# First attention on one core: the attends moved behind the second maximum, the token turn and the first projection

## The chip, the cores and the metric

The kernel runs on one core of a Trainium2 chip. The metric is the device time of one execution in microseconds, the median of the runs shown. The engines are TensorE (PE, with its weight loads as PEld), VectorE (DVE), ScalarE (ACT), GpSimd (POOL) and SyncE (SP). Each works through its own instructions in the order in which they are written, and semaphores join them.

## The reference

Two layers of attention and mixture-of-experts feed-forward on 16 sequences of 256 tokens and 128 features, each part wrapped in layer norms. Only the first attention matters here; it has 16 heads of 8 features and runs two passes, in which the first pass's result is the second pass's query:

```python
        x = (hidden_states - mu) * jax.lax.rsqrt(var + EPS_LN) * ln_w + ln_b
        q = (x @ Wq + bq).reshape(B, S, NH, HD)
        k = (x @ Wk + bk).reshape(B, S, NH, HD)
        v = (x @ Wv + bv).reshape(B, S, NH, HD)
        q = _l2norm(q)
        k = _l2norm(k)
        state = q
        for _ in range(STEPS):
            sim = jnp.einsum('bqhd,bkhd->bqhk', state, k)
            att = jax.nn.softmax(BETA * sim, axis=-1)
            state = jnp.einsum('bqhk,bkhd->bqhd', att, v)
        o = state.reshape(B, S, H) @ Wo + bo
        return residual + o
...
    x = x + _layernorm(_L0_attn_ref(_layernorm(x, axis=-1), ...), axis=-1)
    x = x + _layernorm(_L0_ffn_ref(_layernorm(x, axis=-1), ...), axis=-1)
    x = x + _layernorm(_L1_attn_ref(_layernorm(x, axis=-1), ...), axis=-1)
    x = x + _layernorm(_L1_ffn_ref(_layernorm(x, axis=-1), ...), axis=-1)
    return x
```

## The kernel before

The first attention (`first_attention`) works in units of one sequence (batch b) and four heads: 64 units, one unit started in each step k. In step k, with b = k // 4 and r = k % 4, the engines work on several units at different depths. The order on each engine is written out by hand; a step on TensorE holds:

- op (L449), the output projection of batch b-2, in steps r=3
- S1 (L400): the first pass's scores of unit k into `ps_s`, four banks; ScalarE's exponentials 0 and 1 (L541, `exps`) read it into `p1`
- m0 (L411, `maxima`): the first of four matmuls that score the second pass's queries of unit k-3, for whose maxima VectorE waits (L651). m0, m1, m2 and m3 write the two banks `ps_d` in turn with qp, kp, vp, op, lg, place and O
- yT (L431, r=2): out2 of batch b-2 turned into `ps_a`, copied by ScalarE (L547) between exponentials 0 and 1
- A (L418, `attend`): the attends of units k-6 (second pass, `p2`) and k-1 (first pass, `p1`) into `ps_o`, 16 matmuls written as 32 in the trace. They need last step's exponentials (`exp_done`) and a copied `ps_o` (`o_copied`), and announce `o_full`, on which ScalarE's copy to `ot` (L577) waits
- xT (L431, r=2): the normalised tokens `z1` of batch b+3, turned into `ps_a`. It waits for `z1_ready` (VectorE, L610, shown as a_z) and for ScalarE's copy of yT out of `ps_a`
- qp (L437, r=3): the query projection of batch b+3, read by VectorE at L635
- m1, then S2 (L400): the second pass's scores of unit k-5 into the same `ps_s`, once exponentials 0 and 1 have read it; ScalarE's exponentials 2 and 3 read them
- m2, T (the turned queries, copied by ScalarE between exponentials 2 and 3), lg or place, m3, kp, zT, vp, O (L524, `ot` turned, read by VectorE at L765 to L779), KQ (L425), and S1 of the next step, which waits for exponential 3.

A writer of a `ps_d` bank waits (`wait_d`) until VectorE has read the tile before last: m1 waits for O of the step before in r=0 and r=1, for the reader of m0 where qp stands between them (r=3), for op's reader where it doesn't (r=3 of batches 13 to 15). On VectorE m0's maximum in r=3 stands behind y (L669, reads op) and the scaling of the last projected batch (L686), which needs POOL's powers (L822). A writer of `ps_a` waits (`wait_a`) until ScalarE has copied the tile before. On ScalarE the copy of `ot` (L577) stands ahead of the xT activation (L580) and of exponential 2. Routing work on VectorE (`choose`, `place`) comes at the end of some steps.

Of the kernel before, what the change touches and what calls it, by code (L numbers as in the profile page):

```python
# [20 lines left out]
ACT = mybir.ActivationFunctionType  # L21
# [4 lines left out]
B, S = 16, 256  # L26
# [167 lines left out]
def first_attention(nc, X, Z, ident, a):  # L194
# [22 lines left out]
    def unit(n):  # L217
        return 0 <= n < UNITS
# [4 lines left out]
    with ExitStack() as ctx:  # L223
# [10 lines left out]
        z1 = sb("z1", [P, TPB, D])  # L234
# [23 lines left out]
        xT = sb("xT", [P, S])  # L258
# [10 lines left out]
        ps_o, ps_a = pb("ps_o", [P, 512]), pb("ps_a", [P, 512])  # L269
# [5 lines left out]
        a_full, a_done = sem("a_full"), sem("a_done")  # L275
# [19 lines left out]
        def a_live(k, task):  # L295

            b, r = k // NG, k % NG
            return {"T": unit(k - 2) or unit(k - TURN), "KQ": unit(k + NG),
                    "yT": r == 2 and batch(b - 2), "xT": r == 2 and batch(b + 3),
                    "zT": r == 3 and 0 <= b - 3 < ROUTED}[task]  # L300
# [22 lines left out]
        def a_count(k, task):  # L323
            return a_table[k, task]
# [60 lines left out]
        def _(pe):  # L385
# [6 lines left out]
            def wait_a(st, task):  # L392
                wait(pe, a_done, st.at(lambda k: a_count(k, task) - 1))
# [35 lines left out]
            def transposes(out, parts, done):  # L429
                for t in range(TPB):  # L430
                    last = nc.tensor.transpose(out[:, t * P:(t + 1) * P], parts(t), ident[:, :])  # L431
                last.then_inc(done, 1)
# [8 lines left out]
            for st in steps(pe):  # L441
                k = st.k
                b, r = k // NG, k % NG
                projects = r == 3 and batch(b + 3)
                if d_live(k, "op"):
                    pe.wait_ge(a_done, a_count(k - 1, "yT"))
                    wait_d(st, "op")
                    for t in range(TPB):
                        last = nc.tensor.matmul(narrow(k, "op")[:, t * P:(t + 1) * P], yT[:, t * P:(t + 1) * P],  # L449
                                                a["wo"][:, :], start=True, stop=True)  # L450
                    last.then_inc(d_full, 1)
                if unit(k):
                    pe.wait_ge(a_done, a_count(k - NG, "KQ"))
                    wait(pe, exp_done, exps_of(k - 1, 3))
                    scores(k, q_of(k))
                if unit(k - PEAK):
                    u = k - PEAK
                    pe.wait_ge(kpad_loaded[u % PAD_RING], 64 * (u // PAD_RING + 1))
                    pe.wait_ge(a_done, a_count(k - 1, "T"))
                maxima(st, 0)  # L460
                if a_live(k, "yT"):

                    pe.wait_ge(d_done, d_count(k - 1, "O"))
                    wait_a(st, "yT")
                    transposes(ps_a, lambda t: out2[:, b % 2, t, :], a_full)
                if unit(k - 1) or unit(k - LAST_USE):
                    wait(pe, o_copied, attends(k - 1))
                    pe.wait_ge(exp_done, exps_of(k - 1, 3))
                    if unit(k - LAST_USE):
                        last = attend(k - LAST_USE, p2, 1)  # L470
                    if unit(k - 1):
                        pe.wait_ge(v_ready, k)
                        last = attend(k - 1, p1, 0)
                    last.then_inc(o_full, 1)
                if a_live(k, "xT"):
                    pe.wait_ge(z1_ready, b + 4)
                    wait_a(st, "xT")
                    transposes(ps_a, lambda t: z1[:, t, :], a_full)
                if projects:
                    pe.wait_ge(a_done, a_count(k - 1, "xT"))  # L480
                    project(st, 0, "qp")
                maxima(st, 1)
                if unit(k - SECOND):
                    pe.wait_ge(exp_done, exps_of(k, 1))
                    pe.wait_ge(a_done, a_count(k - 1, "T"))
                    scores(k - SECOND, qs2[:, (k - 1) % 2, S:2 * S])
                maxima(st, 2)
                if a_live(k, "T"):
                    wait_a(st, "T")
                    if unit(k - 2):  # L490
                        pe.wait_ge(qt2_ready, k - 1)
                        last = stack(lambda t: qt2[:, (k - 2) % 4, t * G:(t + 1) * G, :], 0)
                    if unit(k - TURN):
                        pe.wait_ge(d_done, d_count(k - 1, "m3"))
                        last = stack(lambda t: qt2[:, (k - TURN) % 4, t * G:(t + 1) * G, :], 1)
                    last.then_inc(a_full, 1)
                if d_live(k, "lg"):
                    pe.wait_ge(a["later"], 16 * a["laters"])
                    pe.wait_ge(a_done, a_count(k - 1, "zT"))
                    wait_d(st, "lg")  # L500
                    for t in range(TPB):
                        last = nc.tensor.matmul(bank(k, "lg")[:, t * EXPERTS:(t + 1) * EXPERTS],
                                                zT[:, t * P:(t + 1) * P], rt["gate"][:, :], start=True, stop=True)
                    last.then_inc(d_full, 1)
                g = places(k)
                if g is not None:
                    pe.wait_ge(route, ROUTE_SET_UP + ROUTE_LINKS * g + CHOSEN)
                    wait_d(st, "place")
                    place_tokens(nc, bank(k, "place"), rt, GROUPS[g]).then_inc(d_full, 1)
                maxima(st, 3)  # L510
                if projects:
                    project(st, 1, "kp")
                if a_live(k, "zT"):
                    pe.wait_ge(z_new, b - 2)
                    wait_a(st, "zT")
                    transposes(ps_a, lambda t: Z[:, ((b - 3) * TPB + t) * D:((b - 3) * TPB + t + 1) * D], a_full)
                if projects:
                    project(st, 2, "vp")
                if d_live(k, "O"):
                    wait_d(st, "O")  # L520
                    pe.wait_ge(o_copied, attends(k))
                    live = halves(unit(k - 1), unit(k - LAST_USE))
                    for n in range(live.start, live.stop, P):
                        last = nc.tensor.transpose(bank(k, "O")[:, n:n + P], ot[:, n:n + P], ident[:, :])  # L524
                    last.then_inc(d_full, 1)
                if unit(k + NG):
                    nb, g = (k + NG) // NG, r
                    pe.wait_ge(stacks_ready, 2 * (nb + 1))
                    wait_a(st, "KQ")
                    stack(lambda t: kt[:, nb % 2, t * H + g * G:t * H + (g + 1) * G, :], 0)  # L530
                    stack(lambda t: qt[:, nb % 2, t * H + g * G:t * H + (g + 1) * G, :], 1).then_inc(a_full, 1)

        @block.scalar
        def _(act):
# [15 lines left out]
            for st in steps(act):  # L550
# [11 lines left out]
                if r == 3 and batch(b + 2):  # L562

                    act.wait_ge(qk_scaled, b + 3)

                    if batch(b):
                        act.wait_ge(a_full, a_count(k - 4, "KQ"))
                    val, n = scaled[:].rearrange("p a t (h d) -> p a (t h) d", d=HD), TPB * H
                    qd, kd = qt[:, b % 2, :, :], kt[:, b % 2, :, :]
                    nc.scalar.copy(qd[:, :, 0:2 * HD].rearrange("p n (c d) -> p n c d", c=2),  # L570
                                   val[:, 0, :, :].unsqueeze(2).to_broadcast([P, n, 2, HD]))
                    nc.scalar.copy(kd[:, :, 0:4 * HD].rearrange("p n (c d) -> p n c d", c=2)[:, :, :, 0:HD],
                                   val[:, 1, :, :].unsqueeze(2).to_broadcast([P, n, 2, HD])).then_inc(parts_hi, 1)
                if d_live(k, "O"):
                    live = halves(unit(k - 1), unit(k - LAST_USE))
                    act.wait_ge(o_full, attends(k))
                    nc.scalar.copy(ot[:, live], ps_o[:, live]).then_inc(o_copied, 1)  # L577
                if a_live(k, "xT"):
                    act.wait_ge(a_full, a_count(k, "xT"))
                    nc.scalar.activation(xT[:, :], ps_a[:, 0:S], ACT.Identity, scale=a["ln_w"][:, 0:1],  # L580
                                         bias=a["ln_b"][:, 0:1]).then_inc(a_done, 1)
                if unit(k - SECOND):
                    exps(st, 2, k - SECOND, p2)
                if a_live(k, "T"):
# [1980 lines left out]
```

## Time and profile before

| | us |
|---|---|
| median of 3 runs | 1450.89 (1449.8 to 1456.36) |
| span of the profiled execution | 1467.2 |
| its own time outside the profiler | not given |
| PE busy | 1305.1 (89%) |
| DVE busy | 1130.4 (77%) |
| ACT busy | 969.6 (66%) |
| POOL busy | 751.3 (51%) |

The first attention takes about the first 500 us of the span; the other three stages follow. The shares are of the whole span. In the slices of the page between about 70 and 440 us PE stands at 9 tenths or more and the granted clock at full.

### The profile page before, as it was taken

To read this page: it belongs to the slowest core of one execution; us is meant where nothing else is said; L and a number is where in the kernel's file an instruction comes from. 1 tells how busy PE (TensorE), PEld (TensorE's weight loads), DVE (VectorE), ACT (ScalarE), POOL (GpSimd) and SP (SyncE) were. 2 spreads that over 40 slices of the span, in tenths; PEclk is the share of its full clock that TensorE was granted. 3 is DMA by queue.
4 is the path that set the end of the run, shared out by engine and by line. 5 is a ranking of instruction groups with operands and counts; after the bars stand their busy time and mean duration, and the time that the engine had idled before them with its cause. 6 is when DMAs were issued, how large, how long until landed. Compare 5 with 4: busy or idle time off the path is not lost. (4 is left out here: it accounts for less than half of the span.)

```text
span 1467.2 us, 34194 instructions
## 1 busy us (share of the span) xinstructions
PE 1305.1 (89%) x12121; PEld 987.2 (67%) x12121; DVE 1130.4 (77%) x3054; ACT 969.6 (66%) x1498; POOL 751.3 (51%) x961
## 2 busy tenths in 40 slices
PE   2899999999998689899927999999999998699997
PEld 1566666666654367899915777777777776588886
DVE  5578889889875667899956888888888776567776
ACT  1688888888886447777723777777777777343441
POOL 4775665787852363799866455455444220101112
PEclk9899999999998779999958999999999999799999
DMA  6000000111111021122121111111111110134353
GB/s 234 18 23 20 22 20 20 28 32 28 31 36 30 8 80 32 56 73 73 58 87 51 49 47 48 46 48 47 49 46 38 39 42 18 26 92 116 80 129 82
DMA packets 84430, 77.20 MB, mean 53 GB/s; under 512 B 18224, under 2 KB 72240, under 8 KB 83888
## 3 DMA queue, kind: packets, MB, share of 16 engines
q1 hardware_dynamic: 80176, 66.73, 17.1%
q0 software_dynamic: 4096, 8.40, 2.0%
q8 instruction: 95, 1.56, 0.5%
q14 instruction: 63, 0.52, 0.1%
HBM read 36.26 MB, written 13.63 MB: 34 GB/s over the span
## 5 line engine op out<-in xcount | busy, mean ns | idle before, releaser
L541 ACT ACTIVATE a_p<-a_ps_s 128x1024 f32<-128x1024 f32 x256 | 258.3, 1031 | 25.1 <-PE a_ps_s L400 22.2
L651 DVE TENSOR_REDUCE a_qt<-a_ps_d 128x2 fp32r<-128x512 f32 x256 | 174.6, 687 | 48.9 <-PE a_ps_d L411 44.9
L1298 DVE TENSOR_REDUCE a_qt<-a_ps_d 128x2 fp32r<-128x512 f32 x256 | 173.3, 688 | 44.9 <-PE a_ps_d L1086 39.9
L822 POOL TENSOR_TENSOR a_rn<-a_ss,a_half 128x16 f32<-128x16 f32 x56 | 162.6, 2920 | 1.3
L1203 ACT ACTIVATE a_pg<-a_ps_s 128x1024 f32<-128x1024 f32 x128 | 125.8, 1024 | 26.8 <-PE a_ps_s L1075 25.4
L418 PE MATMUL a_ps_o<-a_p,a_v 128*32 128x256 f32 x2048 | 129.5, 393 | 3.7 <-ACT a_p L541 3.7
L1086 PE MATMUL a_ps_d<-a_kpad,a_qs 128*128 128x512 f32 x256 | 126.0, 495 | 5.8 <-DVE a_qt L1298 2.7
L411 PE MATMUL a_ps_d<-a_kpad,a_qs 128*128 128x512 f32 x256 | 126.8, 496 | 4.3 <-DVE a_qt L651 2.4
L2300 ACT ACTIVATE f_s<-f_ps_g 128x512 f32<-128x512 f32 x72 | 43.0, 598 | 99.9 <-PE f_ps_g L2246 99.7
L1494 POOL DMA_INDIRECT a_picked<-ys,rows x64 | 67.6, 1056 | 61.8 <-PE a_ps_d L1086 50.8
L418 PEld LDWEIGHTS a_ps_o<-a_p,a_v 128*32 128x32 f32 x2048 | 61.2, 112 | 52.9 <-issue 22.3
L2050 DVE TENSOR_TENSOR f_sl<-f_s,f_sh 128x512 fp32r<-128x512 f32 x78 | 77.5, 1033 | 10.5 <-ACT f_sh L1929 10.5
L190 POOL DMA_INDIRECT xs<-Z,r_at x64 | 68.5, 1070 | 22.8 <-issue 15.5
L1064 PE MATMUL a_ps_a<-ident,a_qt 128*128 128x128 f32 x512 | 78.3, 276 | 1.4 <-ACT a_kc L1221 0.8
L411 PEld LDWEIGHTS a_ps_d<-a_kpad,a_qs 128*128 128x128 f32 x256 | 48.2, 188 | 40.5 <-issue 13.6
L1225 ACT CAST a_qsm<-a_ps_a 128x512 fp32r<-128x512 f32 x64 | 37.5, 586 | 56.6 <-PE a_ps_a L1064 55.7
L2352 DVE TENSOR_TENSOR f_h<-f_s,f_ps_u 128x512 f32<-128x512 f32 x72 | 48.6, 686 | 32.9 <-PE f_ps_y L2231 19.0
L2231 PEld LDWEIGHTS f_ps_y<-wd,f_p 128*128 128x128 f32 x512 | 63.8, 191 | 9.8 <-DVE f_p L2339 6.9
L2231 PE MATMUL f_ps_y<-wd,f_p 128*128 128x128 f32 x512 | 67.4, 278 | 3.0 <-DVE f_p L2339 2.3
L1086 PEld LDWEIGHTS a_ps_d<-a_kpad,a_qs 128*128 128x128 f32 x256 | 48.3, 190 | 31.3 <-issue 13.5
L1136 PE MATMUL a_ps_o<-a_pg,a_v 128*32 128x256 f32 x1024 | 68.5, 385 | 0.4 <-ACT a_pw L1229 0.4
L1229 ACT ACTIVATE a_pw<-a_ps_s 128x1024 f32<-128x1024 f32 x64 | 66.0, 1031 | 0.1
(355 smaller groups left out, 3823.9 us busy)
## 6 DMA issues: line engine op xcount, KB each, us to landing
a_kpad<-a_kc SPq DMA_DIRECT2D x512, 32.0 KB
f_gb<-spread SPq DMA_DIRECT2D x64, 256.0 KB, 5.7
a_kpad<-a_kq SPq DMA_DIRECT2D x256, 32.0 KB, 1.8
f_xin<-xs SPq DMA_DIRECT2D x39, 128.0 KB, 2.1
ys<-f_yout SPq DMA_DIRECT2D x39, 128.0 KB, 2.1
w<-in_w SPq DMA_DIRECT2D x2, 2304.0 KB, 11.4
out_x<-X SPq DMA_DIRECT2D x8, 256.0 KB, 6.8
xs<-f_zero SPq DMA_DIRECT2D x15, 128.0 KB
```

What stands on the lines that cost most here:

```text
L190: nc.gpsimd.indirect_dma_start(xs, bass.IndirectOffsetOnAxis(rt["at"][:, k, tile:tile + 1], 0), Z[:, tile * D:(tile + 1) * D], None).then_ ...
L411: nc.tensor.matmul(bank(st.k, f"m{part}")[:, :], qs2[:, (st.k - 1) % 2, t * P:(t + 1) * P], kpad[:, u % PAD_RING, 2 * c:2 * c + 2, :].rear ...
L418: last = nc.tensor.matmul(ps_o[SLOT * j:SLOT * (j + 1), half * S:(half + 1) * S], v32[:, u % V_RING, t, j, :], probs[:, u % 2, j, t, :], s ...
L541: nc.scalar.activation(probs[:, u % 2, 2 * c:2 * c + 2, :, :].rearrange("p a b c -> p (a b c)"), ps_s[:, 2 * c:2 * c + 2, :].rearrange("p ...
L651: nc.vector.tensor_reduce(qt2[:, (k - PEAK) % 4, 2 * part:2 * part + 2, SHIFT], bank(k, f"m{part}")[:, :].rearrange("p (a b) -> p a b", b= ...
L822: nc.gpsimd.tensor_tensor(rn[:, part * c:(part + 1) * c], ss[:, part * c:(part + 1) * c], half[:, 0:c], ALU.pow).then_inc(rn_ready, 1)
L1064: last = nc.tensor.transpose(ps_a[:, n:n + P], stacked(src[:, (u // NG) % 2, kind, t * H + t0:t * H + t0 + G, :]), ident[:, :])
L1086: nc.tensor.matmul(bank(k, f"m{part}")[:, :], qs[:, k % 2, t * P:(t + 1) * P], kpad[:, k % PAD_RING, GLOBAL, 2 * c:2 * c + 2, :].rearrange ...
L1203: nc.scalar.activation(pg[:, u % 2, 2 * c:2 * c + 2, :, :].rearrange("p a b c -> p (a b c)"), ps_s[:, 2 * c:2 * c + 2, :].rearrange("p a b ...
L1298: nc.vector.tensor_reduce(qt[:, b % 2, GLOBAL, n:n + 2, SHIFT], bank(k, f"m{part}")[:, :].rearrange("p (j s) -> p j s", s=S), AX.X, ALU.ma ...
L2050: nc.vector.tensor_tensor(sl[:, half_of(n, h)], s[:, half_of(n, h)], sh[:, half_of(n, h)].bitcast(F32), ALU.subtract).then_inc(sl_done, 1)
L2231: last = nc.tensor.matmul(ps_y[:, t * D:(t + 1) * D], src, a["wd"][:, q * D:(q + 1) * D], start=q == 0 and t == 0, stop=q == NQ - 1 and t ...
```

## The change

The edit moves two blocks. On TensorE, xT, qp and m1 are written ahead of the attends, which now stand directly ahead of S2. On ScalarE, the activation that copies xT is written ahead of the copy of `ot`. Its lines are numbered L576 and L581 afterwards.

```diff
--- before.py
+++ after.py
@@ -463,6 +463,14 @@
                     pe.wait_ge(d_done, d_count(k - 1, "O"))
                     wait_a(st, "yT")
                     transposes(ps_a, lambda t: out2[:, b % 2, t, :], a_full)
+                if a_live(k, "xT"):
+                    pe.wait_ge(z1_ready, b + 4)
+                    wait_a(st, "xT")
+                    transposes(ps_a, lambda t: z1[:, t, :], a_full)
+                if projects:
+                    pe.wait_ge(a_done, a_count(k - 1, "xT"))
+                    project(st, 0, "qp")
+                maxima(st, 1)
                 if unit(k - 1) or unit(k - LAST_USE):
                     wait(pe, o_copied, attends(k - 1))
                     pe.wait_ge(exp_done, exps_of(k - 1, 3))
@@ -472,14 +480,6 @@
                         pe.wait_ge(v_ready, k)
                         last = attend(k - 1, p1, 0)
                     last.then_inc(o_full, 1)
-                if a_live(k, "xT"):
-                    pe.wait_ge(z1_ready, b + 4)
-                    wait_a(st, "xT")
-                    transposes(ps_a, lambda t: z1[:, t, :], a_full)
-                if projects:
-                    pe.wait_ge(a_done, a_count(k - 1, "xT"))
-                    project(st, 0, "qp")
-                maxima(st, 1)
                 if unit(k - SECOND):
                     pe.wait_ge(exp_done, exps_of(k, 1))
                     pe.wait_ge(a_done, a_count(k - 1, "T"))
@@ -571,14 +571,14 @@
                                    val[:, 0, :, :].unsqueeze(2).to_broadcast([P, n, 2, HD]))
                     nc.scalar.copy(kd[:, :, 0:4 * HD].rearrange("p n (c d) -> p n c d", c=2)[:, :, :, 0:HD],
                                    val[:, 1, :, :].unsqueeze(2).to_broadcast([P, n, 2, HD])).then_inc(parts_hi, 1)
+                if a_live(k, "xT"):
+                    act.wait_ge(a_full, a_count(k, "xT"))
+                    nc.scalar.activation(xT[:, :], ps_a[:, 0:S], ACT.Identity, scale=a["ln_w"][:, 0:1],
+                                         bias=a["ln_b"][:, 0:1]).then_inc(a_done, 1)
                 if d_live(k, "O"):
                     live = halves(unit(k - 1), unit(k - LAST_USE))
                     act.wait_ge(o_full, attends(k))
                     nc.scalar.copy(ot[:, live], ps_o[:, live]).then_inc(o_copied, 1)
-                if a_live(k, "xT"):
-                    act.wait_ge(a_full, a_count(k, "xT"))
-                    nc.scalar.activation(xT[:, :], ps_a[:, 0:S], ACT.Identity, scale=a["ln_w"][:, 0:1],
-                                         bias=a["ln_b"][:, 0:1]).then_inc(a_done, 1)
                 if unit(k - SECOND):
                     exps(st, 2, k - SECOND, p2)
                 if a_live(k, "T"):
```

TensorE, from S1 to S2 of a step r=2. a_out is out2 (yT), a_z the normalised tokens (xT), a_p and a_v the probabilities and values of the attends. Before:

```order
L400 MATMUL a_ps_s<-a_kq 128x256 x8
L411 MATMUL a_ps_d<-a_kpad,a_qs 128x512
L431 MATMUL a_ps_a<-ident,a_out 128x128 x2
L418 MATMUL a_ps_o<-a_p,a_v 32x256 x16
L431 MATMUL a_ps_a<-ident,a_z 128x128 x2
L411 MATMUL a_ps_d<-a_kpad,a_qs 128x512
L400 MATMUL a_ps_s<-a_qs,a_kq 128x256 x8
```

After:

```order
L400 MATMUL a_ps_s<-a_kq 128x256 x8
L411 MATMUL a_ps_d<-a_kpad,a_qs 128x512
L431 MATMUL a_ps_a<-ident,a_out 128x128 x2
L431 MATMUL a_ps_a<-ident,a_z 128x128 x2
L411 MATMUL a_ps_d<-a_kpad,a_qs 128x512
L418 MATMUL a_ps_o<-a_p,a_v 32x256 x16
L400 MATMUL a_ps_s<-a_qs,a_kq 128x256 x8
```

The two turns into `ps_a` now follow each other directly, and the attends have moved behind the turn of a_z and behind m1.

TensorE, from S1 to S2 of the step r=3 that follows. a_xT and wqkv make the first projection. Before:

```order
L400 MATMUL a_ps_s<-a_kq 128x256 x8
L411 MATMUL a_ps_d<-a_kpad,a_qs 128x512
L418 MATMUL a_ps_o<-a_p,a_v 32x256 x16
L437 MATMUL a_ps_d<-wqkv,a_xT 128x128 x2
L411 MATMUL a_ps_d<-a_kpad,a_qs 128x512
L400 MATMUL a_ps_s<-a_qs,a_kq 128x256 x8
```

After:

```order
L400 MATMUL a_ps_s<-a_kq 128x256 x8
L411 MATMUL a_ps_d<-a_kpad,a_qs 128x512
L437 MATMUL a_ps_d<-wqkv,a_xT 128x128 x2
L411 MATMUL a_ps_d<-a_kpad,a_qs 128x512
L418 MATMUL a_ps_o<-a_p,a_v 32x256 x16
L400 MATMUL a_ps_s<-a_qs,a_kq 128x256 x8
```

Three writers of the `ps_d` banks (m0, qp, m1) now follow each other with nothing between, and the attends come behind them. VectorE's, POOL's and SP's orders stay the same.

ScalarE, from exponential 0 to exponential 2 of a step r=2. Before:

```order
L541 ACTIVATE a_p<-a_ps_s 128x1024
L547 COPY a_yT<-a_ps_a 128x256
L541 ACTIVATE a_p<-a_ps_s 128x1024
L577 COPY a_ot<-a_ps_o 128x512
L580 ACTIVATE a_xT<-a_ps_a,ln_b,ln_w 128x256
L541 ACTIVATE a_p<-a_ps_s 128x1024
```

After:

```order
L541 ACTIVATE a_p<-a_ps_s 128x1024
L547 COPY a_yT<-a_ps_a 128x256
L541 ACTIVATE a_p<-a_ps_s 128x1024
L576 ACTIVATE a_xT<-a_ps_a,ln_b,ln_w 128x256
L581 COPY a_ot<-a_ps_o 128x512
L541 ACTIVATE a_p<-a_ps_s 128x1024
```

The copy of `ot` now comes directly ahead of exponential 2.

## Rows read from the trace of the kernel before

**Rows 1.** The page: span; costliest groups (busy, mean ns | idle before, releaser).

```profile
span 1467.2 us, 34194 instructions
...
L651 DVE TENSOR_REDUCE a_qt<-a_ps_d 128x2 fp32r<-128x512 f32 x256 | 174.6, 687 | 48.9 <-PE a_ps_d L411 44.9
```

**Rows 2.** Busy time by stretch: one batch, and the stage's thin end.

```profile
core 0: us, PE busy (x) PEld busy (x) DVE busy (x) ACT busy (x) POOL busy (x), PEclk, DMA share, GB/s
155.24:182.25 27.01, 26.37 (x283) 17.40 (x283) 22.88 (x76) 23.65 (x34) 17.43 (x17) 1.00 0.09 21
...
450.00:500.00 50.00, 40.35 (x373) 23.12 (x373) 31.89 (x111) 28.08 (x40) 15.04 (x18) 0.88 0.08 23
```

**Rows 3.** Timeline of a step r=2 (start us, duration us, engine, line, operation).

```profile
155.24 0.51 PE L400 MATMUL a_ps_s<-a_kq 32*128 32x256 f32 x8 [0.30 <-ACT a_p L541]
...
156.32 1.93 PE L418 MATMUL a_ps_o<-a_p,a_v 128*32 128x256 f32 x32
...
156.52 0.60 DVE L610 TENSOR_SCALAR a_z<-Z,a_mv_b,a_rs_b 128x128 f32<-128x128 f32 x2 [0.49 <-POOL a_rs_b L818]
156.71 0.37 ACT L547 COPY a_yT<-a_ps_a 128x256 f32<-128x256 f32 x1
...
158.19 0.44 PE L431 MATMUL a_ps_a<-ident,a_z 128*128 128x128 f32 x2
...
158.38 0.47 PE L411 MATMUL a_ps_d<-a_kpad,a_qs 128*128 128x512 f32 x1
...
159.34 1.02 ACT L541 ACTIVATE a_p<-a_ps_s 128x1024 f32<-128x1024 f32 x1
```

**Rows 4.** Timeline of a step r=2 behind routing work: S1 and z.

```profile
346.15 0.50 PE L400 MATMUL a_ps_s<-a_kq 32*128 32x256 f32 x8 [0.30 <-ACT a_p L541]
...
348.14 0.64 DVE L610 TENSOR_SCALAR a_z<-Z,a_mv_b,a_rs_b 128x128 f32<-128x128 f32 x2
```

**Rows 5.** Timeline of the step r=3 that follows the one in rows 3.

```profile
162.00 0.51 PE L400 MATMUL a_ps_s<-a_kq 32*128 32x256 f32 x8
...
162.56 1.94 ACT L541 ACTIVATE a_p<-a_ps_s 128x1024 f32<-128x1024 f32 x2 [0.30 <-PE a_ps_s L400]
...
162.66 0.41 DVE L669 TENSOR_TENSOR a_y<-a_ps_d,Z 128x256 f32<-128x256 f32 x1
...
162.87 1.93 PE L418 MATMUL a_ps_o<-a_p,a_v 128*32 128x256 f32 x32
162.99 0.91 DVE L686 TENSOR_TENSOR a_scaled<-a_qk,a_rn 128x512 f32<-128x512 f32 x1
163.82 0.68 DVE L651 TENSOR_REDUCE a_qt<-a_ps_d 128x2 fp32r<-128x512 f32 x1
...
164.73 0.71 PE L437 MATMUL a_ps_d<-wqkv,a_xT 128*128 128x128 f32 x4
...
165.20 0.48 PE L411 MATMUL a_ps_d<-a_kpad,a_qs 128*128 128x512 f32 x1
...
165.60 0.51 PE L400 MATMUL a_ps_s<-a_qs,a_kq 32*128 32x256 f32 x8
165.89 2.06 DVE L651 TENSOR_REDUCE a_qt<-a_ps_d 128x2 fp32r<-128x512 f32 x3
...
166.04 0.50 PE L411 MATMUL a_ps_d<-a_kpad,a_qs 128*128 128x512 f32 x1
166.16 1.02 ACT L541 ACTIVATE a_p<-a_ps_s 128x1024 f32<-128x1024 f32 x1 [0.16 <-PE a_ps_s L400]
```

**Rows 6.** Timeline of the step r=0 that follows.

```profile
170.02 0.51 PE L411 MATMUL a_ps_d<-a_kpad,a_qs 128*128 128x512 f32 x1
170.10 0.21 DVE L779 TENSOR_TENSOR a_out<-a_ps_d,a_ro 128x64 f32<-128x64 f32 x1
...
170.45 1.93 PE L418 MATMUL a_ps_o<-a_p,a_v 128*32 128x256 f32 x32
...
172.45 0.59 ACT L577 COPY a_ot<-a_ps_o 128x512 f32<-128x512 f32 x1 [0.34 <-PE a_ps_o L418]
...
173.31 1.02 ACT L541 ACTIVATE a_p<-a_ps_s 128x1024 f32<-128x1024 f32 x1 [0.27 <-PE a_ps_s L400]
```

## The prediction

> **What bounds the kernel now.** The page comes first: the span, and one group of the first attention, where all of the change lies: VectorE's 256 maxima cost 174.6 us, and VectorE stood idle 44.9 us ahead of them for their matmul [rows 1]. No engine is simply full, so the order of hand-overs decides. The busy times by stretch say the same: in one batch of four steps (27.01 us) PE shows 26.37, ACT 23.65, DVE 22.88 us, and the granted clock is 1.00 [rows 2]. PE's ends are modelled, so its 98% is partly waiting in the pipeline. The page's chain of waits covers only the program's end and says nothing here; the timeline of single steps must be read instead, one step of each kind (r = k mod 4) [rows 3, 5, 6].
>
> The loop that closes each step is: scores S1 of step k, two exponentials; TensorE meanwhile runs m0, the attends (A) and m1; then the second pass's scores S2, which need both first exponentials and free `ps_s`; then exponential 2, the turned copy, exponential 3, and S1 of the next step. In the step r=0 A starts 0.43 after m0 (170.45 against 170.02) and lasts 1.93; the copy of `ot` starts at 172.45, 0.07 behind its end, takes 0.59, and exponential 2 starts at 173.31 [rows 6]. So from A's start to exponential 2 are 2.86 us, and the two first exponentials (1.94 together [rows 5]) are over before that. TensorE's in-order queue between S1 and S2 therefore sets the step, and whatever TensorE waits for there lengthens it.
>
> **What the change does, step by step.** No instruction is added or taken away. m1, in r=2 the token turn xT, and in r=3 the first projection qp, go from behind A to ahead of it. A needs nothing that is late (exponentials of earlier steps, a copied `ps_o`), so before the change it is 1.9 us of work that runs while the inputs of xT, qp and m1 are made. Afterwards TensorE waits for those with nothing to fill the time. SP, POOL and VectorE keep their order; only their waits on A (`o_full`) and on m1 shift.
>
> Plain order cost. After: m1 0.43 (the m0-to-A distance), then A, whose end plus 0.07 starts the copy of `ot` (2.00 from A's start [rows 6]), 0.59 for the copy. Exponential 2 stands behind that copy on ACT. Back to back, ACT starts about 0.1 before the former row's end (the pair of 1.02 to 1.04 lasts 1.94 [rows 5]). So 0.43 + 2.00 + 0.49 = 2.92 from the end of m0's slot, against 2.86: **+0.06** for each step. Before, m1 and S2 hid this copy; now it is as long as S2 with its 0.56 to exponential 2 (165.60 to 166.16 [rows 5]). That is all that r=1 pays.
>
> r=0: m1 writes the bank that transposed `ot` of the step before occupied, and VectorE leaves it when L779 ends, 170.31. m1's new slot is 170.45, so the wait is over by about 0.1: +0.06 more for a semaphore. **+0.12**.
>
> r=2: xT and yT share `ps_a`, so xT must wait until ACT has copied yT, and ACT has an exponential ahead of that copy; the copy ends at 156.71 + 0.37 = 157.08. z, its input, ends at 156.52 + 0.60 = 157.12 [rows 3]. xT can start at 157.17, where A used to run from 156.32 to 158.25. Then m1 0.19 later (158.19 to 158.38), A 0.43 after that, 157.79. Copy of `ot` 159.79 to 160.38, exponential 2 at 160.28 against 159.34: **+0.94**. ACT's activation of xT, now before the copy of `ot`, ends near 158.5 and costs nothing, since ACT waits for A there.
>
> r=3: m1 writes the bank after m0 and qp: in this ring each matmul waits for the reader of the last but one, and that is m0's maximum. On VectorE this maximum stands behind L669 (ends 163.07) and the scaling L686 and ends at 163.82 + 0.68 = 164.50 [rows 5]. So m1 moves to 164.55 at the earliest, A to 164.98, where it stood at 162.87. A's end plus 0.07 is 166.98, copy to 167.57, exponential 2 at 167.47 against 166.16: **+1.31**. S2 and m2 are late by 1.24 (164.98 + 1.86, the distance 162.87 to 164.73, is 166.84, against 165.60). VectorE's three maxima from 165.89 to 167.95 don't absorb this: the second and third now wait for m2, 166.04 + 1.24 + 0.50 = 167.78, and end 1.4 later, at 169.2.
>
> Sum of a full batch: 0.06 + 0.12 + 0.94 + 1.31 = 2.43 us. qp is live for batches 0 to 12, xT too; the first two lack yT or part of A, and I count them as full, since z at 1.88 behind S1 holds xT there [rows 3]: 13 x 2.43 = 31.6. Batches 13 to 15 have no qp and no xT; in r=3 m1 waits only for L669 (S1 + 1.07, m1 at 1.12 in place of 0.87), +0.31 with the 0.06, and the other steps 0.24: 3 x 0.55 = 1.7. After a group's routing work on VectorE z comes later: 348.78 behind an S1 of 346.15, 2.63 in place of 1.88 [rows 4]; two batches with a live xT have this: 2 x 0.75 = 1.5. Together +34.8 us.
>
> This stands against the profiled execution, span 1467.2 us; its own time outside the profiler isn't given, and the span is 16.3 above the median of 1450.89. Scaled with 1450.89/1467.2 = 0.989 the loss is 34.4, so **1485.3 us**.
>
> Bounds. From below: S2 alone counts (+1.24, +0.88 in r=2, 0 in r=0 and r=1), 13 x 2.12 = 27.6, that is 1478. From above: in r=3 the whole 1.93 of A comes on top, since it then stands fully behind m1, 13 x 0.62 = 8.1 more, and r=2 may have z late by 0.75 in 9 more batches, 6.8: 34.8 + 14.9 = 49.7, that is 1500. None of the moves takes less than nothing on TensorE, since the same instructions run in sequence between S1 and S2; a gain could come only through VectorE, which gets m1 earlier (rival 2).
>
> **Rivals.**
> 1. Part of the delay is taken up behind it. In r=3 S1 of the next step is started by TensorE's queue of projections, transposes and stacks. If that queue had slack, r=3's 1.31 would vanish: 34.8 - 17.0 = 17.8, 1468.5. Against it: that queue waits for the third maximum, which moves by 1.4 as worked out. And m2 follows S2.
> 2. Faster. VectorE is the limit, and m1's early result gives back its idle time: 44.9 us ahead of the maxima [rows 1], of which the half that belongs to m1 and what follows it, 22, would go: 1429. It decides only where T or the O transposes, and not the exponentials, hold the next S1; DVE with 22.88 of 27.01 us busy [rows 2] and a maximum for m1 that was waiting in r=3 for qp speaks a little for it. Against: m1 can't start in r=2 and r=3 before z or m0's maximum, which are VectorE's own work.
> 3. Collisions pile up: z and m0's maximum come 0.75 late in every batch as they do in [rows 4], because POOL's powers and scatters and VectorE's tail shift against each other. 9 x 0.75 + 13 x 0.75 = 16.5 more, 51.3 x 0.989 = 50.7: 1501.6.
> 4. The clock falls. With TensorE waiting some 0.5 to 0.9 us in r=2 and r=3 the clock could be granted as in the thin end of the stage, 0.88 with 40.35 of 50 us busy [rows 2]. The queue from S1 to S2, 3.60 us in r=3 [rows 5], would take 0.12/0.88 = 14% longer, 0.50 in each of 64 steps, 32 more: (34.8 + 32) x 0.989 = 66.1, 1517. The Trainium skill (TensorE: Matmul & The Clock Gate, Part 1) holds that TensorE falls to its lower clock when it has been idle for a while; by that rule the order that fills the waits is the safer one. The trace agrees at the thin end, and no row shows whether pauses under 1 us do it.
> 5. The order makes no difference: A and the rest only change places. Then 1451. The waits above would have to be wrong; the row order shows that the moves do happen.
>
> **How the numbers follow.** The forecast has 0.64, rival 1 0.10, rival 2 0.06, rival 3 0.10, rival 4 0.04, rival 5 0.06. The forecast's own 1478 to 1500, with rivals 1 and 3, gives a range of 1466 to 1508. 0.5% is 7.3 us, about what a measurement of this kernel can tell from no change. Faster 0.06, within 0.06, slower 0.88.
>
> **What would show it.** In a step r=2: xT right behind the end of yT's copy, TensorE idle before it, A 1.4 to 1.5 us later after S1 than before. In r=3: m1 0.05 behind m0's maximum, A 2.98 behind S1 (0.87 before). In r=0 and r=1: A some 0.5 later than before, the copy of `ot` ending where exponential 2 starts, and exponential 2 waiting for it rather than for S2. A batch takes about 29.4 in place of 27.0 us. DVE's idle time ahead of the maxima grows. The forecast is wrong if S1-to-S2 grows as said but the batch doesn't, or if m0's maximum in r=3 ends earlier after S1.

## The result and the profile after

The changed kernel takes 1488.71 us, the median of 4 runs (1486.9 to 1490.59); the kernel before 1450.93 (1449.8 to 1456.36). The medians differ by 37.8 us. The ratio is 1.0247, 95% interval 1.0219 to 1.0274, which is 31.8 to 39.8 us of 1450.9.

The profiled execution shown ahead had a span of 1467.2 us with a stall of 5 us near 465 us and a slow stretch behind it, which a second profile of the same kernel (below, span 1447.0) doesn't have; the steps named in the prediction are the same in both within 0.02 us, and sums over whole stages are taken from the second.

The page of the changed kernel, as [rows 1]:

```profile
span 1488.8 us, 34194 instructions
...
L651 DVE TENSOR_REDUCE a_qt<-a_ps_d 128x2 fp32r<-128x512 f32 x256 | 173.6, 686 | 93.6 <-PE a_ps_d L411 92.5
...
L581 ACT COPY a_ot<-a_ps_o 128x512 f32<-128x512 f32 (+1 forms) x69 | 38.4, 556 | 76.1 <-PE a_ps_o L418 76.1
```

VectorE's idle time ahead of the maxima has doubled, from 44.9 to 92.5 us, and ScalarE now stands 76.1 us ahead of the copy of `ot`, where it stood 29.5 before. Neither engine has more work: the maxima take 173.6 us against 174.6. Both wait for TensorE, whose attends come later.

Busy time by stretch, as [rows 2]: one batch of four steps, then a stretch behind routing work, both of the changed kernel:

```profile
core 0: us, PE busy (x) PEld busy (x) DVE busy (x) ACT busy (x) POOL busy (x), PEclk, DMA share, GB/s
160.17:189.01 28.84, 26.58 (x282) 17.38 (x283) 22.60 (x77) 23.39 (x34) 17.30 (x17) 1.00 0.08 20
240.00:270.00 30.00, 26.19 (x255) 15.84 (x256) 21.23 (x78) 20.97 (x30) 13.81 (x13) 0.89 0.08 19
```

The batch takes 28.84 us in place of 27.01, with busy times that differ by 0.3 us at most: 1.8 us of waiting were added. In the second stretch the granted clock is 0.89, where the kernel before had 1.00.

The step r=2, timeline, as [rows 3]:

```profile
160.17 0.51 PE L400 MATMUL a_ps_s<-a_kq 32*128 32x256 f32 x8 [0.30 <-ACT a_p L541]
...
161.39 0.60 DVE L610 TENSOR_SCALAR a_z<-Z,a_mv_b,a_rs_b 128x128 f32<-128x128 f32 x2 [0.49 <-POOL a_rs_b L818]
161.65 0.37 ACT L547 COPY a_yT<-a_ps_a 128x256 f32<-128x256 f32 x1
...
162.16 0.41 PE L431 MATMUL a_ps_a<-ident,a_z 128*128 128x128 f32 x2 [0.83 <-ACT a_yT L547]
162.32 0.47 PE L411 MATMUL a_ps_d<-a_kpad,a_qs 128*128 128x512 f32 x1
162.73 1.93 PE L418 MATMUL a_ps_o<-a_p,a_v 128*32 128x256 f32 x32
...
164.73 0.59 ACT L581 COPY a_ot<-a_ps_o 128x512 f32<-128x512 f32 x1 [1.34 <-PE a_ps_o L418]
...
165.21 1.03 ACT L541 ACTIVATE a_p<-a_ps_s 128x1024 f32<-128x1024 f32 x1
```

TensorE stands 0.83 us until yT is copied (161.65 + 0.37 = 162.02), and only then runs the token turn, m1 and the attends. The attends start 2.56 behind S1, where they started 1.08 behind it. Exponential 2 starts 5.04 behind S1 against 4.10 before: +0.94.

The step r=3 that follows, as [rows 5]:

```profile
167.40 0.72 POOL L848 TENSOR_TENSOR Z<-Z,bo 128x256 f32<-128x256 f32 x1
...
167.87 0.50 PE L400 MATMUL a_ps_s<-a_kq 32*128 32x256 f32 x8
...
168.86 0.68 DVE L686 TENSOR_TENSOR a_scaled<-a_qk,a_rn 128x512 f32<-128x512 f32 x1
169.08 0.68 PE L437 MATMUL a_ps_d<-wqkv,a_xT 128*128 128x128 f32 x4 [0.28 <-DVE a_y L669]
169.46 0.68 DVE L651 TENSOR_REDUCE a_qt<-a_ps_d 128x2 fp32r<-128x512 f32 x1
...
170.19 0.50 PE L411 MATMUL a_ps_d<-a_kpad,a_qs 128*128 128x512 f32 x1 [0.43 <-DVE a_qt L651]
...
170.63 1.93 PE L418 MATMUL a_ps_o<-a_p,a_v 128*32 128x256 f32 x32
...
172.49 0.51 PE L400 MATMUL a_ps_s<-a_qs,a_kq 32*128 32x256 f32 x8
...
173.11 1.03 ACT L541 ACTIVATE a_p<-a_ps_s 128x1024 f32<-128x1024 f32 x1
```

m1 starts at 170.19, 0.05 behind the end of m0's maximum (170.14). The attends start 2.76 behind S1, in place of 0.87, and exponential 2 5.24, in place of 4.16: +1.08.

The step r=0 that follows, up to the S1 of the step r=1, TensorE's rows only, as [rows 6]:

```profile
176.51 0.51 PE L400 MATMUL a_ps_s<-a_kq 32*128 32x256 f32 x8
176.95 0.79 PE L411 MATMUL a_ps_d<-a_kpad,a_qs 128*128 128x512 f32 x2
177.68 1.93 PE L418 MATMUL a_ps_o<-a_p,a_v 128*32 128x256 f32 x32
179.54 0.51 PE L400 MATMUL a_ps_s<-a_qs,a_kq 32*128 32x256 f32 x8
...
182.84 0.51 PE L400 MATMUL a_ps_s<-a_kq 32*128 32x256 f32 x8
```

Here nothing is lost: S2 comes 3.03 behind S1, against 3.16 before, and the whole step takes 6.33 against 6.38 us. From m0's start the attends start 0.73 later, behind two maxima matmuls, not twice 0.43.

One step behind routing work (r=2) of the changed kernel:

```profile
246.49 0.51 PE L400 MATMUL a_ps_s<-a_kq 32*128 32x256 f32 x8 [0.30 <-ACT a_p L541]
...
248.41 0.60 DVE L610 TENSOR_SCALAR a_z<-Z,a_mv_b,a_rs_b 128x128 f32<-128x128 f32 x2
...
249.07 0.65 PE L431 MATMUL a_ps_a<-ident,a_z 128*128 128x128 f32 x2 [1.42 <-DVE a_z L610]
...
250.08 3.13 PE L418 MATMUL a_ps_o<-a_p,a_v 128*32 128x256 f32 x32
...
253.14 0.51 PE L400 MATMUL a_ps_s<-a_qs,a_kq 32*128 32x256 f32 x8
```

z is late, TensorE waits 1.42 us, and then the attends take 3.13 us in place of 1.93: behind the longer wait they ran at the lower of TensorE's two clocks (1.2 GHz; the granted clock of 249.2 to 252.5 is 0.50), and the next scores at the full one again (2.4 GHz). S1 to S2 is 6.65 us, where the kernel before had 3.55.

A wait of this length doesn't always bring the lower clock. The next step r=2 of the changed kernel waits 1.41 us and keeps the full clock:

```profile
283.83 0.44 PE L431 MATMUL a_ps_a<-ident,a_z 128*128 128x128 f32 x2 [1.41 <-DVE a_z L610]
...
284.42 1.93 PE L418 MATMUL a_ps_o<-a_p,a_v 128*32 128x256 f32 x32
```

### The profile page after: what moved, and what is told of

It is laid out like the page before. It is cut to its first block and busy times, and to the rows that moved or that the text cites. A ratio compares the mean times of both kernels' runs of the same rounds, so it can differ in the third digit from the quotient of the medians.

```text
span 1488.8 us, 34194 instructions
## 1 busy us (share of the span) xinstructions
PE 1309.6 (88%) x12121; PEld 991.0 (67%) x12121; DVE 1126.9 (76%) x3054; ACT 967.9 (65%) x1498; POOL 751.2 (50%) x961
## 5 line engine op out<-in xcount | busy, mean ns | idle before, releaser
L651 DVE TENSOR_REDUCE a_qt<-a_ps_d 128x2 fp32r<-128x512 f32 x256 | 173.6, 686 | 93.6 <-PE a_ps_d L411 92.5
L418 PE MATMUL a_ps_o<-a_p,a_v 128*32 128x256 f32 x2048 | 135.1, 406 | 3.3 <-ACT a_p L541 3.3
L1086 PE MATMUL a_ps_d<-a_kpad,a_qs 128*128 128x512 f32 x256 | 126.9, 499 | 3.5 <-DMA a_kpad<-a_kc 1.2
L411 PE MATMUL a_ps_d<-a_kpad,a_qs 128*128 128x512 f32 x256 | 120.4, 489 | 10.3 <-DVE a_qt L651 7.2
L581 ACT COPY a_ot<-a_ps_o 128x512 f32<-128x512 f32 (+1 forms) x69 | 38.4, 556 | 76.1 <-PE a_ps_o L418 76.1
```

Source lines behind the costliest of these rows:

```text
L411: nc.tensor.matmul(bank(st.k, f"m{part}")[:, :], qs2[:, (st.k - 1) % 2, t * P:(t + 1) * P], kpad[:, u % PAD_RING, 2 * c:2 * c + 2, :].rear ...
L418: last = nc.tensor.matmul(ps_o[SLOT * j:SLOT * (j + 1), half * S:(half + 1) * S], v32[:, u % V_RING, t, j, :], probs[:, u % 2, j, t, :], s ...
L651: nc.vector.tensor_reduce(qt2[:, (k - PEAK) % 4, 2 * part:2 * part + 2, SHIFT], bank(k, f"m{part}")[:, :].rearrange("p (a b) -> p a b", b= ...
L1086: nc.tensor.matmul(bank(k, f"m{part}")[:, :], qs[:, k % 2, t * P:(t + 1) * P], kpad[:, k % PAD_RING, GLOBAL, 2 * c:2 * c + 2, :].rearrange ...
```

## The experiments

All ratios are against the kernel before on the same chip, 1451.6 to 1452.5 us (11 to 23 runs). "Less" is against the 1488.7 us of the changed kernel.

**One kind of step put back.** In the changed kernel the attends are written as a function and called early in some steps.

```diff
+                early = r == 2
+                if early:
+                    attend_both()
                 if a_live(k, "xT"):
...
                 maxima(st, 1)
+                if not early:
+                    attend_both()
```

> The changed kernel, with the steps r=2 put back into the old order (attends, token turn, m1; ScalarE's token copy behind the copy of ot). Theory (TensorE waits in r=2 for yT's copy or z, with the attends behind the wait): the 0.9 us of each of 13 steps r=2 and the slow-clock steps they start go away, about 18 us: 1471 us, and scores to scores in r=2 back at 3.55 us. Rival (the cost is spread evenly over all steps, by ScalarE's copy of ot standing exposed): only a quarter of 38 us goes, 1479. Rival (r=2 only takes up slack that r=3 then has to wait for anyway): unchanged, 1487 to 1490.

Measured: 1475.42 us (ratio 1.0178, 1.0155 to 1.0200), 13.3 less than the changed kernel. S1 to S2 in r=2 is back at 3.55. But in r=3 it rose from 4.62 to 4.84 to 4.86 in four ordinary steps, and in two more (at 310 and 339 us) from 4.52 to 5.28 and 6.58: there the scaling stood 0.58 us for POOL's powers, and the second of them had the lower clock. That is part of why 13 and not 18 us came back. The timeline of such a step shows VectorE's scaling at 0.91 us, where the changed kernel had 0.68:

```profile
167.02 0.73 POOL L854 TENSOR_TENSOR Z<-Z,bo 128x256 f32<-128x256 f32 x1
...
167.39 0.91 DVE L692 TENSOR_TENSOR a_scaled<-a_qk,a_rn 128x512 f32<-128x512 f32 x1
```

POOL's addition of `bo` runs from 167.02 to 167.75 and meets the scaling. In the kernel before it met it as well (0.91 at [rows 5]):

```profile
162.62 0.73 POOL L848 TENSOR_TENSOR Z<-Z,bo 128x256 f32<-128x256 f32 x1
```

In the changed kernel it ended at 168.12, before the scaling began at 168.86.

With `early = r == 3`:

> The changed kernel, with the steps r=3 put back into the old order (attends, qp, m1). Theory (m1 waits there for m0's maximum, with the attends behind the wait): 1.05 us in each of 13 steps and the slow-clock steps they start go away, about 20 us: 1469 us, and scores to scores in r=3 back at 3.60 us. Rival (even spread over all steps): 1479. Rival (slack only moved): 1487 to 1490.

Measured: 1465.39 us (1.0101, 1.0084 to 1.0118), 23.3 less where some 20 were expected; S1 to S2 in ordinary steps r=3 is 3.60 again.

With `early = r >= 2`, so that m1 is ahead of the attends in r=0 and r=1 alone:

> Both r=2 and r=3 in the old order: m1 is ahead of the attends in r=0 and r=1 alone. By the prediction's working (0.12 and 0.06 us more a step): 1451 + 3 = 1454. By the changed kernel's trace, where these steps take 0.05 to 0.12 us less: 1448 to 1449. If waits in r=2 and r=3 carry the whole loss, it is within 5 us of the kernel before, and the granted clock of 200 to 400 us is 1.00 again.

Measured: 1451.78 us, ratio 1.0002 (0.9984 to 1.0021). The two parts add up: 1488.7 - 13.3 - 23.3 = 1452.1. So r=2 costs some 13 us, r=3 some 23 us, waits and lower clock together, and r=0 and r=1 nothing that can be measured. The exposed copy of `ot`, which stands there in every step, costs these steps no more than m1's new place gives back. The granted clock of this version:

```profile
200.00:300.00 100.00, 96.67 (x1050) 64.30 (x1041) 86.10 (x289) 86.29 (x121) 70.78 (x62) 1.00 0.10 23
300.00:400.00 100.00, 96.71 (x1048) 64.04 (x1045) 85.74 (x279) 85.38 (x119) 79.56 (x75) 1.00 0.12 31
```

**Filling the wait with useless work.**

```diff
+                if r >= 2 and (a_live(k, "xT") or projects) and unit(k - LAST_USE):
+                    wait(pe, o_copied, attends(k - 1))
+                    pe.wait_ge(exp_done, exps_of(k - 1, 3))
+                    attend(k - LAST_USE, p2, 1)
                 if a_live(k, "xT"):
```

> The changed kernel with work added and none taken away: in steps r=2 and r=3 the second-pass half of the attends (8 matmuls, about 1 us) is run once more ahead of the token turn or the first projection, as a filler, and then overwritten by the real one. Theory (in the steps behind routing work TensorE waits over 1 us and the granted clock then falls, which costs some 13 us): the attends of those steps take 1.93 again in place of 3.1, and the time falls to about 1477 in spite of the added work. Rival (those steps are long because their inputs are late, and the clock costs nothing of its own): 1489 to 1495.

Measured: 1482.69 us (1.0227, 1.0209 to 1.0245), 6 less than the changed kernel although TensorE does more: the trace has 2432 rows of attend matmuls against 2048, that is 24 fillers of 16 rows. The trace has no lower clock between 64 and 520 us. The stretch that had 0.89 now has the full one, and its attends behind the late z take 1.93 us:

```profile
240.00:270.00 30.00, 28.12 (x314) 17.95 (x308) 23.65 (x79) 23.31 (x34) 17.17 (x16) 1.00 0.08 19
...
252.83 0.44 PE L431 MATMUL a_ps_a<-ident,a_z 128*128 128x128 f32 x2 [0.50 <-DVE a_z L614]
...
253.44 1.93 PE L418 MATMUL a_ps_o<-a_p,a_v 128*32 128x256 f32 x32
```

Step by step against the changed kernel, S1 to S2 of five steps with the lower clock went from 6.65, 6.99, 6.64, 7.83 and 6.74 to 5.13, 5.55, 5.34, 6.47 and 5.26: 7.1 us. The filler itself costs 0.14 in the ordinary steps r=2. What is left above 4.5 in those five steps is the late input, not the clock. The expected 13 us for the clock was too much; it is about 7, and 1.6 more at the stage's end.

**Making m0's maximum earlier in r=3.** On VectorE, `maxima(0)` is called ahead of the scaling in those steps:

```diff
+                if r == 3:
+                    maxima(0)
                 if r == 3 and batch(b + 2):
                     dve.wait_ge(rn_ready, 4 * (b + 3))
...
-                maxima(0)
+                if r != 3:
+                    maxima(0)
```

> The changed kernel, with m0's maximum ahead of the scaling on VectorE in the steps r=3 (VectorE's order alone is changed). Theory (in r=3 m1 and the attends wait for m0's maximum): it ends 0.6 us earlier, scores to scores in r=3 go from 4.62 to about 4.05 us, 13 steps give 7 to 8 us and fewer steps run at the lower clock: 1477 to 1482. Rival (m1 in r=3 is held by something else, the projection or the weights): no change, 1487 to 1490.

Measured: 1480.23 us (1.0195, 1.0167 to 1.0222), 8.5 less. Timeline of a step r=3:

```profile
166.34 0.51 PE L400 MATMUL a_ps_s<-a_kq 32*128 32x256 f32 x8
...
167.34 0.68 DVE L651 TENSOR_REDUCE a_qt<-a_ps_d 128x2 fp32r<-128x512 f32 x1
167.56 0.68 PE L437 MATMUL a_ps_d<-wqkv,a_xT 128*128 128x128 f32 x4 [0.29 <-DVE a_y L669]
...
168.07 0.50 PE L411 MATMUL a_ps_d<-a_kpad,a_qs 128*128 128x512 f32 x1
168.50 1.93 PE L418 MATMUL a_ps_o<-a_p,a_v 128*32 128x256 f32 x32
```

The maximum ends at 168.02 and m1 starts at 168.07. The wait was indeed for m0's maximum; a change in the order of VectorE alone moved TensorE's attends by 0.6 us. S1 to S2 is 4.02.

This trace also has the step shown above that waited 1.41 us and kept its clock. Here it waits as long, and its attends run at the lower one:

```profile
278.34 0.44 PE L431 MATMUL a_ps_a<-ident,a_z 128*128 128x128 f32 x2 [1.41 <-DVE a_z L610]
...
278.94 3.06 PE L418 MATMUL a_ps_o<-a_p,a_v 128*32 128x256 f32 x32
```

S1 to S2 is 6.53 us in place of 5.41. So which of the late steps meets the lower clock differs from version to version, by 1.1 to 1.6 us a step, and the times above and below hold some of that.

**Cutting the attends in two.** The second-pass half stays ahead of the token turn and qp, the first-pass half comes behind m1:

```diff
+                if unit(k - LAST_USE):
+                    last = attend(k - LAST_USE, p2, 1)
+                    if not unit(k - 1):
+                        last.then_inc(o_full, 1)
...
                 maxima(st, 1)
+                if unit(k - 1):
+                    pe.wait_ge(v_ready, k)
+                    attend(k - 1, p1, 0).then_inc(o_full, 1)
```

> The order of the changed kernel, except that the attends are cut in two in every step: the second-pass half (8 matmuls, about 1 us) stays ahead of the token turn and the first projection, the first-pass half comes behind m1. Theory (only TensorE's waits with nothing to fill them cost time): the first half covers the wait for yT's copy and for m0's maximum (0.8 and 0.7 us), so TensorE hardly waits, the clock stays, and the time is that of the kernel before within 4 us: 1447 to 1455. Rival (having attends directly ahead of the second pass's scores costs by itself, since ScalarE's copy of ot then stands bare ahead of exponential 2): 0.1 us or more in 64 steps on top, 1458 or more.

Measured: 1472.16 us (1.0131, 1.0103 to 1.0159). The expectation of 1447 to 1455 fell, and the rival's reason is only part of it. The waits in r=2 are gone as expected (S1 to S2 3.68) and the clock stayed at 1.00 from 100 to 500 us, but two other things came. In r=0 and r=1 S1 to S2 rose to 3.30, from 3.03 and 2.97 in the changed kernel:

```profile
326.47 1.07 PE L418 MATMUL a_ps_o<-a_p,a_v 128*32 128x256 f32 x16
327.47 0.49 PE L411 MATMUL a_ps_d<-a_kpad,a_qs 128*128 128x512 f32 x1
327.90 1.07 PE L418 MATMUL a_ps_o<-a_p,a_v 128*32 128x256 f32 x16
328.90 0.51 PE L400 MATMUL a_ps_s<-a_qs,a_kq 32*128 32x256 f32 x8
```

Each half takes 1.00 from its start to the next instruction, 2.00 for both, where the whole took 1.86, and m1 between the halves costs 0.43 again. And in r=3 S1 to S2 took 4.20: TensorE's wait ahead of m1 is down to 0.18 us, but m1 comes late all the same and the second half behind it:

```profile
167.48 0.79 POOL L849 TENSOR_TENSOR Z<-Z,bo 128x256 f32<-128x256 f32 x1
167.59 0.76 DVE L794 TENSOR_TENSOR a_qt<-a_state,a_qt 128x64 fp32r<-128x64 f32 x1
...
169.21 0.68 DVE L652 TENSOR_REDUCE a_qt<-a_ps_d 128x2 fp32r<-128x512 f32 x1
```

Here POOL's addition meets another instruction of VectorE, the subtraction L794, which takes 0.76 us in place of 0.23 and holds up everything behind it; m0's maximum ends 2.71 behind an S1 at 167.18, in the changed kernel 2.27. The exposed copy of `ot` shows as well, as 0.07 us from S2 to the next S1 (3.20 against 3.13).

**Moving the routing work on VectorE.** In the changed kernel `choose` goes from the end of a step to just ahead of m2's maximum:

```diff
                 maxima(1)
+                for g, (first, last) in enumerate(GROUPS[:-1]):
+                    part = k - (NG * (last + 3) + PLACE_STEP)
+                    if part == -4:
+                        dve.wait_ge(d_done, d_count(NG * (last + 4), "lg"))
+                    if -4 <= part < -1:
+                        choose(nc, link, rt, GROUPS[g], part - (-4))
                 maxima(2)
```

> The changed kernel, with the routing work on VectorE (choose, three parts of 2 to 5 small instructions in the steps r=1, 2 and 3 of four batches) moved within the step from its end to just ahead of m2's maximum, where VectorE stands idle for 2 us in r=2 and r=3. Theory (some 14 of the 38 us are steps behind routing work, where z and op's reader come late, TensorE waits longer and the clock falls): z and the reader of op are on time again, the long steps (5.1 to 7.8 us from scores to scores) go back to 4.4 to 4.6, the clock is 1.00: 1476 to 1480. Rival (the clock falls from the ordinary waits of 0.8 us as well, and the late inputs are chance): 1485 to 1490.

Measured: 1480.32 us (1.0198, 1.0181 to 1.0215), 8.4 less; 9 to 13 had been expected. The stretch that had 0.89 is at full clock, and its steps r=2 and r=3 take 4.79 and 4.73 from S1 to S2 in place of 6.65 and 6.99. Two long steps (6.97 and 7.23) are left; they stand behind `place` and not behind `choose`. Their waits for z are what they were (1.40 and 1.60 us, against 1.41 and 1.60), but in the changed kernel they kept the full clock (5.41 and 5.60) and here they have the lower one; the last stretch below holds the first of them:

```profile
240.00:270.00 30.00, 26.67 (x285) 17.30 (x282) 24.72 (x87) 23.78 (x34) 17.52 (x17) 1.00 0.08 19
280.00:300.00 20.00, 19.17 (x194) 12.16 (x195) 13.34 (x40) 13.59 (x20) 11.30 (x13) 0.92 0.09 22
```

**Looking for a faster version.** The same move in the kernel before, ahead of qp's reader and with the parts one step later:

> The kernel before, with the same routing work placed ahead of m1's maximum in the steps r=2, 3 and 0, where VectorE waits for m1 or qp by 1.2 and 1.05 us. The first profile has four to six steps of 0.4 to 0.75 us too much behind routing work. Theory: 1 to 3 us faster than before, 1448 to 1450. Rival (VectorE's work there pushes m1's maximum and with it the later ones): 0 to 3 us slower.

Measured: 1452.93 us, ratio 1.0004 (0.9993 to 1.0015): no change, where 1 to 3 us had been expected. One step r=3 became 0.77 us shorter from S1 to S2 (4.37 to 3.60), and another became 1.1 us longer behind S2 (3.98 to 5.12).

And `early = r >= 2 or k < 8`:

> The kernel with both r=2 and r=3 in the old order, and r=0 and r=1 too for the first eight steps, in which the trace of the version with m1 ahead lost 2 us. Theory (from the ninth step on each r=0 and r=1 is 0.06 us shorter on the mean, as that trace shows): 1449 to 1450, 0.1% faster than before. Rival: what m1 gains on TensorE is given back elsewhere: 1451 to 1452.

Measured: 1452.31 us, ratio 1.0003 (0.9994 to 1.0013): no change, nearer to the rival of the expectation than to its theory. m1 ahead of the attends in r=0 and r=1 is worth nothing that can be measured, so no version here beats the kernel before.

**The kernel before once more.**

> The kernel before once more, for a second profile. The first one had a span of 1467.2 us against a median of 1450.9, with a stall of 5.5 us between 460.8 and 469.4 us that the other traces don't have. If that is chance of one execution, the span is 1449 to 1452 and S1 to S2 and S2 to S1 repeat those of the first profile (3.17, 3.13; 3.16, 3.13; 3.55, 3.21; 3.60, 3.98). If it belongs to profiling, the span is again above 1460.

Measured: 1448.78 us in one run, and the page's first line:

```profile
span 1447.0 us, 34194 instructions
```

The stall was chance of one execution. Against this profile the last S1 of the changed kernel is at 496.02 in place of 461.69 us, 34.3 later, and the last S2 at 526.03 in place of 488.58, 37.4 later. The spans differ by 41.8, so 37.4 of it arises in the first attention; the 4.4 behind it lie in stages whose instructions are the same, and the runs of the kernel before alone spread from 1448.5 to 1459.4 us.

## Why the prediction was right, point by point

The forecast was 1485.3, with its range 1466 to 1508; measured 1488.7. The mechanism was right: the waits of xT and m1, which the attends used to cover. That the sum came so close is luck in part: the ordinary steps were put too high (31.6 us, some 21 measured), and what comes on top of them too low (3.2 us, some 16 measured).

- **r=2, +0.94**: measured +0.94 to exponential 2, and the step 7.70 us against 6.76. The order of the releases was as worked out (yT's copy 162.02, z 161.99, xT 162.16). All steps r=2 of the changed kernel lose 16.6 us over the two traces, 8.0 of it the four late ones; putting them back gives 13.3, since steps r=3 became longer. The first batches, counted as full, lost less: all steps of the first three 3.4 us together.
- **r=3, +1.31**: the place was right, m1 0.05 behind m0's maximum, and making the maximum earlier moved it. The size was off: measured +1.08. m0's maximum ended 2.27 behind S1, not 2.50, since the scaling L686 took 0.68 in place of 0.91 us, no longer meeting POOL's addition of `bo`. The term that was mis-sized is m0's maximum, carried over from a trace in which POOL stood elsewhere. The prediction had named an earlier end of this maximum as a sign of being wrong; it was one, worth 0.23 us a step. Even in the kernel before only four steps r=3 have the stretched scaling (136.04, 162.99, 190.00 and 216.94); one of them was taken for all. Four timelines agree (0.91 with the meeting in the kernel before and with r=2 put back, 0.68 without it, and 0.76 for 0.23 where the addition met L794). Over all the traces here, each of the 30 scalings that began during an addition took 0.90 to 1.24 us, and all but one of the 129 that met none 0.67 to 0.75. No experiment moved POOL's addition alone. One slip has no part in the sum: the third maximum, by the prediction's own figures (169.2 against 167.95), ends 1.25 later and not 1.4; measured is 1.00.
- **r=0 and r=1, +0.12 and +0.06**: measured -0.05 and -0.12, the other way. The exposed copy of `ot` is there as 0.07 from S2 to S1 (3.20 against 3.13), but m1 right behind m0 costs 0.24 to 0.30 and not the 0.43 of the m0-to-A distance, and it no longer stands between A and S2. The version with this part alone has the time of the kernel before.
- **The sum of a batch, 2.43**: measured 1.83 (28.84 against 27.01). 13 such batches make 23.8 us, where the prediction had 31.6; with the first batches as they are, and without what lateness adds, it is some 21.
- **What lay outside**: the prediction had 1.5 us for late z behind routing work and 1.7 for the last batches. Step by step against the second profile of the kernel before, z, the reader of op or m0's maximum is late in eight steps and not in two, and in five of them the clock falls as well. These eight steps lose 21.4 us, 13.4 more than ordinary ones would; 7.1 of that is the clock, the rest the late input. The stretch from the last S1 to the last S2 adds 3.1 us, 1.6 of it clock. All other steps lose 12.9. That is rivals 3 and 4, which the prediction gave 0.10 and 0.04, each at a part of its price: moving `choose` gave back 8.4 us, and filling the waits 7.1 us of clock (the two overlap). Rival 3 was reckoned for every batch; it came in four steps r=2 and four r=3. Rival 4 was reckoned as a clock of 0.88 through all 64 steps; it is full clock in most, and the lower one in five and in the last.
- **Rival 1** (r=3 taken up behind it) is out: undoing r=3 gave 23.3 us. **Rival 2** (VectorE's idle time comes back) is out: that idle time doubled. **Rival 5** (no difference) is out by the ratio.
- **The clock**: ordinary waits of 0.83 us (r=2) and 0.28 + 0.43 us (r=3) left the granted clock at 1.00 through whole batches. Behind longer ones it fell in some steps and not in others: of the fourteen steps r=2 that waited 1.40 to 1.60 us for z (four each in the changed kernel, with r=3 put back and with the maximum first, two with `choose` moved), seven ran their attends at the lower clock, and the same step did so in one version and not in another. With the filler in place, which left 0.41 to 0.60 us of these waits, none did. By the rule of the Trainium skill (TensorE: Matmul & The Clock Gate, Part 1) that idle time brings the lower clock, the trace agrees for a part of the long waits, and the short ones show that it isn't any pause. What decides among the long ones no run here shows.

What stays open: how far the lateness behind `place` (two steps at 6.97 and 7.23) can be taken away, and whether POOL's addition alone, moved away from VectorE's scaling, gives the 0.23 us. A token turn into a free half of `ps_a` wasn't tried; it could gain little in an ordinary step, since z itself ends at 161.99 and yT's copy at 162.02.

## What to carry to other kernels

In an in-order queue, long work whose inputs are ready is the cover for instructions whose inputs come late; before moving it, ask for each instruction that goes ahead of it when its last input lands, counting from the step's start, and charge the difference once for each step of that kind. Check the reader of the buffer as well as the maker of the data: here the wait for a maximum behind unrelated work on VectorE (r=3, some 23 us) cost more than the wait for an input (r=2, some 13). And after the sum, look at the steps in which those inputs are late already: there the new wait is longest, and it can cost the matmul clock on top (8 of 63 steps made over half of the 37.4 us here).

## What the runs showed of the hardware

- VectorE's instructions with two inputs in SBUF were stretched where a POOL addition of 0.73 to 0.79 us had begun before them and still ran: 0.91 for 0.68, and 0.76 for 0.23. Where VectorE had begun first, the addition was the one that took longer (1.17 in place of 0.73 us at 81.61 in the kernel before, beside a scaling of 0.72 that began at 81.47). The Trainium skill (SBUF — State Buffer, SBUF: two separate sides) tells of a port pair that the two engines share as an exclusive lock; the trace agrees that one of them is held up, the one that began later.
- One wait of 1.42 us on TensorE was followed by attends of 3.13 us in place of 1.93. The same step with a wait of 1.41 us had 1.93 in one version and 3.06 in another. Eight more matmuls in each of 24 waits, overwritten later, kept the full clock and made the kernel 6 us faster.
- Cutting 16 attends into two groups of 8 with one 128x512 matmul between them takes 2.00 in place of 1.86 us for the attends.
- A second 128x512 maxima matmul right behind the first pushes the attends by 0.24 (r=1) to 0.30 us (r=0, in some steps 0.36); the first pushes them by 0.43.
